# One maximum over sixteen heads and one subtraction: merging two halves in a top-k attention layer

## The chip, the cores and the metric

The kernel runs on one core of one Trainium2 chip. The metric is the device time of one execution in microseconds; a kernel's time is the median of its runs.

## The reference, cut to what matters

The program is a transformer of four layers on `x` of 64 sequences x 128 tokens x 128 features, with a context of 64 x 77 x 128. Each layer adds a cross attention and a feed-forward part, both on the layer-normed `x`. The change lies in the cross attention of the last layer, which has low-rank projections and keeps only the 64 largest of 77 scores:

```python
qh = _heads(_lowrank_proj(q, Uq, Vq, bq), B, L)      # 16 heads of 8
kh = _heads(_lowrank_proj(k, Uk, Vk, bk), B, S)      # S = 77
vh = _heads(_lowrank_proj(v, Uv, Vv, bv), B, S)
scores = jnp.einsum('bhld,bhsd->bhls', qh, kh) * SCALE
flat = scores.reshape(-1, S)
vals, idx = jax.lax.top_k(flat, 64)
p = jax.nn.softmax(vals, axis=-1)
attn = jnp.zeros_like(flat).at[rows, idx].set(p)     # back in shape b h l s
out = jnp.einsum('bhls,bhsd->bhld', attn, vh)
```

The feed-forward part behind it is a mixture of 64 experts; each token goes to its four likeliest, and each expert takes at most 128 of them.

## The kernel before, in words

`attention_layer` works one sequence of 128 tokens per step, tokens on the 128 partitions, and writes 64 such steps out as straight code. Each engine has its own list, and the lists meet only at semaphores. In step `s` an engine works on several sequences at once: the scores of sequence `s`, the selection of `s-1`, the probabilities of `s-2` (`lag` is 2), the output of later stages. The tiles have two halves, taken in turn (`u`), so sequence `s` reuses the buffers of `s-2`.

Sixteen heads of 77 scores are 1232 numbers per token. TensorE puts them into four PSUM banks of four heads. ScalarE copies them in two halves of eight heads (616 numbers) into `a_T` (`copy_scores`, L565, signals `copied0` and `copied1`). VectorE finds the maximum of each head (`subtract_max`, L696, into `a_mx`, signals `mx0` and `mx1`). GpSimd writes "maximum minus score", a distance, over the scores (`distances`, L630, signals `distance0` and `distance1`).

To keep 64 of 77, the 13 largest distances are thrown out, in two rounds of MAX8 (the eight largest of a row) and MATCH_REPLACE8 (put a huge negative number where they stand): `select_eight` (L727), `replace_eight` (L735), `select_rest` (L743), a memset of three of the second eight (L751) and `replace_rest` (L756). Each is 16 instructions, one per head, of 77 elements. TensorE then turns the result, ScalarE takes the absolute value and exp(-distance), and TensorE weighs the values.

VectorE's list in step `s` of this layer is, in order (the names in brackets belong to the router and exist in one step of four):

```
select_eight(s-1), residual(s-4), [minima], replace_eight(s-1),
subtract_max(s, half 0), norm_heads(s-3), select_rest(s-1), place_v(s+1),
[sums | best | keys_in_order], statistics(s-4), [best_four],
subtract_max(s, half 1), [reciprocals | marks], replace_rest(s-1)
```

`norm_heads` (L676, L681) divides the weighed values by the sums of the probabilities; `place_v` (L774) lays out the values of the next sequence.

GpSimd's list in step `s` is: the router's `pool_first`, `distances` for half 0 and half 1, `add_bias` (L618), the router's `pool_end`.

The router of the feed-forward part runs inside these steps, for groups of four sequences. With `c = s // 4` and `v = s % 4`, `pool_first` does `probabilities(c-3)` and `deviations(c-2)` at `v` = 0 and `place(c-3)` at `v` = 2. `place` (L2613 to L2629) computes for each token the row that each chosen expert has for it, and ends in `e3r_skey` (L2626) and `e3r_wf` (L2629). VectorE's `keys_in_order` (L2725) takes the four largest of `e3r_skey` in the same step. `pool_end` does `chosen` at `v` = 0, `fill_rows` at `v` = 2, and in every step a `scatter` (L2645) of four indirect DMAs, at `v` of 0 and 1 from the fifth group of steps on. After the last attention step the router goes on for a few groups alone. The context for each sequence comes by SyncE's DMAs (L314), which wait for `proj`.

Of the kernel before, what the change touches and what calls it, by code (L numbers as in the profile page):

```python
# [9 lines left out]
ALU = mybir.AluOpType  # L10
ACT = mybir.ActivationFunctionType
AX = mybir.AxisListType.X
# [17 lines left out]
def real(i, n=B):  # L30

    return not isinstance(i, int) or 0 <= i < n


def past(i, back):

    return not isinstance(i, int) or i >= back
# [39 lines left out]
def bcast(ap, axis, n):  # L77

    a = ap.unsqueeze(axis)
    shape = list(a.shape)  # L80
    shape[axis] = n
    return a.broadcast_to(shape)
# [45 lines left out]
def attention_layer(nc, m, k, w, heads, keys, scale, context=None, mask=None, topk=0, lowrank=False,  # L128
# [21 lines left out]
    k_ready = "k_by_scalar" if topk else "k"  # L150
    sfree = "copied" if topk else "sfree"
# [4 lines left out]
    q = m.at  # L156
    with ExitStack() as ctx:
# [10 lines left out]
        y = sb("y", [S, 2, D])  # L168
        yT = sb("yT", [D, 2, S])
# [4 lines left out]
        mx = sb("mx", [S, 2, heads])  # L174
        T = sb("T", [S, 2, heads * keys])
        Pr = sb("Pr", [keys, 2, heads * S])
        oT = sb("oT", [D, 2, wide])
# [430 lines left out]
        @block.gpsimd  # L608
        def _(pool):
            norm_gpsimd_rest(pool, m)  # L610
            if y_by_scalar:
                offsets(pool, 2, slice(FIRST, B))

            def add_bias(i, u):
                pool.wait_ge(q["y"], q.nth("y", i))
                xi = m.X[:, bass.ds(i, 1), :].rearrange("p a d -> p (a d)")
                if inner is None:
                    pool.tensor_tensor(xi, xi, bo[:, :], ALU.add).then_inc(q["bias"], 1)  # L618
                else:
                    pool.wait_ge(q["yraw"], q.nth("yraw", i))  # L620
                    pool.tensor_tensor(y0[:, u, :], y0[:, u, :], bo[:, :], ALU.add).then_inc(q["y0"], 1)
                    pool.wait_ge(q["y0"], q.nth("y0", i))
                    pool.tensor_tensor(xi, xi, y0[:, u, :], ALU.add).then_inc(q["bias"], 1)

            def distances(i, u, half):

                t3 = T[:, u, :].rearrange("p (k h c) -> p k h c", k=2, c=keys)[:, half, :, :]
                m3 = mx[:, u, :].rearrange("p (k h) -> p k h", k=2)[:, half, :]
                pool.wait_ge(q[f"mx{half}"], q.nth(f"mx{half}", i))
                pool.tensor_tensor(t3, bcast(m3, 2, keys), t3, ALU.subtract).then_inc(q[f"distance{half}"], 1)  # L630

            def less_maxima(i, u, half):

                t3 = T[:, u, :].rearrange("p (k h c) -> p k h c", k=2, c=keys)[:, half, :, :]
                m3 = mx[:, u, :].rearrange("p (k h) -> p k h", k=2)[:, half, :]
                pool.wait_ge(q[f"mx{half}"], q.nth(f"mx{half}", i))
                pool.tensor_tensor(t3, t3, bcast(m3, 2, keys), ALU.subtract).then_inc(q[f"T{half}"], 1)  # L637

            def step(s, v, h):
                u, a = v % 2, (v + 1) % 2  # L640
                if inner is not None and real(s + 1):
                    pool.wait_ge(q["yT"], q.nth("yT", s + 1))
                    if past(s + 1, 2):
                        pool.wait_ge(q["proj"], q.nth("proj", s + 1, 2))

                    pool.tensor_tensor(yT[:, a, :], xw[:, a, :], m.WIDTH_FEATURES[:, :], ALU.mult) \
                        .then_inc(q["xT"], 1)
                if real(s):
                    if mask is not None:
                        for half in range(2):  # L650
                            less_maxima(s, u, half)
                    if router is not None:
                        router.pool_first(pool, s)
                    if topk:
                        for half in range(2):
                            distances(s, u, half)
                    add_bias(s, u)
                elif router is not None:
                    router.pool_first(pool, s)
                if router is not None:  # L660
                    router.pool_end(pool, s)
            run_written_out(pool, step, 2, max(0, beyond), slots=slots)
            if router is not None:
                router.pool_last(pool)

        @block.vector
        def _(dve):
# [16 lines left out]
            def subtract_max(i, u, h, half):  # L684

                banks = slice(2 * half, 2 * half + 2)
                raw = PS[:, banks, 0:hpg * keys].rearrange("p g (a c) -> p g a c", c=keys)
                t4 = T[:, u, :].rearrange("p (g a c) -> p g a c", a=hpg, c=keys)[:, banks, :, :]
                t3 = T[:, u, :].rearrange("p (k h c) -> p k h c", k=2, c=keys)[:, half, :, :]
                m4 = mx[:, u, :].rearrange("p (g a) -> p g a", a=hpg)[:, banks, :]  # L690
                m3 = mx[:, u, :].rearrange("p (k h) -> p k h", k=2)[:, half, :]
                if topk:
                    dve.wait_ge(q[f"copied{half}"], q.nth(f"copied{half}", i))
                    if past(i, 2):
                        dve.wait_ge(q[f"distance{half}"], q.nth(f"distance{half}", i, 2))
                    dve.tensor_reduce(m3, t3, AX, ALU.max).then_inc(q[f"mx{half}"], 1)  # L696
                    return
                dve.wait_ge(q["scores"], q.nth("scores", i))
                if past(i, 2):
                    turned = f"PT{turns // 2 * (half + 1) - 1}"  # L700
                    dve.wait_ge(q[turned], q.nth(turned, i, 2))
                if mask is not None:
                    dve.wait_ge(q[f"mask{u}"], h * 16 + (16 + mask_base))
                    for g in range(2):
                        last = dve.scalar_tensor_tensor(
                            out=t4[:, g, :, :], in0=bcast(mk[:, u, :], 1, hpg), scalar=-1.0e9,
                            in1=raw[:, g, :, :], op0=ALU.mult, op1=ALU.add)
                    last.then_inc(q[f"sfree{half}"], 1)
                    dve.wait_ge(q[f"sfree{half}"], q.nth(f"sfree{half}", i))
                    if past(i, 2):  # L710
                        dve.wait_ge(q[f"T{half}"], q.nth(f"T{half}", i, 2))
                    dve.tensor_reduce(m3, t3, AX, ALU.max).then_inc(q[f"mx{half}"], 1)  # L712
                    return
                dve.tensor_reduce(m4, raw, AX, ALU.max).then_inc(q[f"mx{half}"], 1)  # L714
                dve.wait_ge(q[f"mx{half}"], q.nth(f"mx{half}", i))
                dve.tensor_tensor(t4, raw, bcast(m4, 3, keys), ALU.subtract).then_inc(q[f"sfree{half}"], 1)  # L716

            def select_eight(i, u):
                t3 = T[:, u, :].rearrange("p (h c) -> p h c", c=keys)


                for h in range(heads):
                    if h % (heads // 2) == 0:
                        half = h // (heads // 2)
                        dve.wait_ge(q[f"distance{half}"], q.nth(f"distance{half}", i))
                        pass_wait()
                    last = dve.max(r1[:, u, 8 * h:8 * h + 8], t3[:, h, :])  # L727
                last.then_inc(q["r1"], 1)
# [63 lines left out]
            def step(s, v, h):  # L792
                u, a = v % 2, (v + 1) % 2
                end, fin = s - lag - 1, s - lag - 2
                if topk:
# [6 lines left out]
                        router.vector_first(dve, s)  # L802
                    if real(s - 1):
                        replace_eight(s - 1, a)
                    if real(s):
                        subtract_max(s, u, h, 0)
                    if real(end):
                        norm_heads(end, (v - lag - 1) % 2)
                    if real(s - 1):
# [7 lines left out]
                    if router is not None:  # L817
                        router.vector_fourth(dve, s)
                    if real(s):
                        subtract_max(s, u, h, 1)  # L820
                    if router is not None:
                        router.vector_last(dve, s)
                    if real(s - 1):
# [25 lines left out]
                    router.vector_last(dve, s)  # L849
            run_written_out(dve, step, 2, max(lag + 2, beyond), slots=slots)  # L850

        used = ["y", "yTps", "yT", "proj", "projv", "q", k_ready, "v", "scores", f"{sfree}0", f"{sfree}1", "mx0", "mx1",
                "pv", "oT", "back", "rec", "O", "OTps", "OT", "out", "bias", "x"]
        used += [f"{n}{g}" for n in ("PT", "P") for g in range(turns)]
        used += ["distance0", "distance1"] if topk else []
        used += ["T0", "T1"] if less_max == "T" else []
        used += ["xT"] if inner is not None else []
        for n in used:
# [2192 lines left out]
def program(nc, t):  # L3051
    with ExitStack() as ctx:
# [3 lines left out]
        def sem(name):  # L3056
# [26 lines left out]
        m.at = Signals(ctx, nc, "at", [  # L3083
# [5 lines left out]
            "y0", "yraw", "irstd", "cut", "mr", "nmr", "in_sq", "in_var", "in_mr", "in_nmr"])  # L3089
# [147 lines left out]
```

## Time and profile before

| | us |
|---|---|
| median of 3 runs | 3944.61 |
| lowest and highest | 3942.61, 3950.3 |
| the profiled execution | 3949.06 |
| its span, first to last instruction | 3947.3 |
| attention of layer 3 in that span, about | 2710 to 3634 |

The profile is that of one execution. Busy time is the time in which an engine worked on instructions; a record can overlap its successor on the same engine, so on an engine without idle time the distance from start to start is what adds up. PE is TensorE, DVE is VectorE, ACT is ScalarE, POOL is GpSimd. An idle time in square brackets stands ahead of the instruction of its line, with the one that released it.

### The profile page before, as it was taken

How to read it: one execution, taken by the hardware profiler on the slowest of the kernel's cores; microseconds unless marked ns; L12 is line 12 of the kernel's file. 1: busy time of each engine (PE TensorE's matmuls, PEld its weight loads, DVE VectorE, ACT ScalarE, POOL GpSimd, SP SyncE). 2: the span in 40 equal slices, each digit the busy share in tenths (PEclk: the TensorE clock that was granted, in tenths of full speed). 3: DMA queues.
4: the chain of work that ended last, by engine and by line, in shares of the span. 5: the costliest groups of instructions: out<-in, count | busy, mean ns of one | idle time of the engine just before them, and what ended most of it. 6: DMA issues, size and time to landing. Idle time of an engine off the chain costs nothing. (4 is left out here: it accounts for less than half of the span.)

```text
span 3947.3 us, 77991 instructions
## 1 busy us (share of the span) xinstructions
PE 3004.5 (76%) x23435; PEld 1888.8 (48%) x23435; DVE 3014.5 (76%) x12267; ACT 2240.8 (57%) x4368; POOL 1905.5 (48%) x2166
## 2 busy tenths in 40 slices
PE   3777776999979997797599968885777767777069
PEld 1222222444447776443467745554555555555046
DVE  6999997666667776344788858887999999998065
ACT  4999997333346665242366646664666666665030
POOL 5777776000014566575444442222256666666660
PEclk9999998999989999898799979996555665655585
DMA  2000000940000010253200000000011100000037
GB/s 74 5 5 5 5 6 22 418 193 0 0 16 17 27 29 26 79 140 111 61 15 15 15 8 2 2 2 13 20 36 38 38 18 5 5 5 2 1 111 213
DMA packets 161015, 177.77 MB, mean 45 GB/s; under 512 B 71762, under 2 KB 136180, under 8 KB 153179
## 3 DMA queue, kind: packets, MB, share of 16 engines
q1 hardware_dynamic: 127964, 140.65, 11.7%
q0 software_dynamic: 23424, 27.94, 2.1%
q10 hardware_dynamic: 9216, 4.20, 0.4%
q8 instruction: 197, 3.23, 0.3%
q14 instruction: 214, 1.75, 0.1%
HBM read 80.48 MB, written 113.61 MB: 49 GB/s over the span
## 5 line engine op out<-in xcount | busy, mean ns | idle before, releaser
L395 PE MATMUL PS<-IDENT,a_T 128*77 128x128 f32 (+1 forms) x3584 | 618.3, 313 | 132.0 <-ACT a_Pr L540 110.5
L1037 ACT ACTIVATE l_H<-l_H 128x2048 f32<-128x2048 f32 (+2 forms) x256 | 597.3, 2702 | 2.8 <-POOL l_H L1089 2.6
L395 PEld LDWEIGHTS PS<-IDENT,a_T 128*77 128x77 f32 (+1 forms) x3584 | 487.0, 171 | 226.8 <-ACT a_Pr L540 88.6
L1089 POOL TENSOR_TENSOR l_H<-l_feat,l_text 128x4096 f32<-128x4096 f32 x64 | 450.4, 7039 | 131.5 <-PE PS L993 130.8
L993 PE MATMUL PS<-l_H,l_wide 128*32 128x512 f32 (+1 forms) x2560 | 332.2, 595 | 165.3 <-ACT l_H L1037 165.3
L1111 DVE TENSOR_TENSOR l_H<-PS,l_text 128x2048 f32<-128x2048 f32 (+1 forms) x192 | 411.7, 2146 | 2.1 <-ACT l_text L1064 2.1
L542 ACT ACTIVATE a_Pr<-PS 77x512 f32<-77x512 f32 (+1 forms) x640 | 375.4, 588 | 59.4 <-PE PS L395 59.4
L412 PE MATMUL PS<-a_Pr,a_vaug 77*32 77x128 f32 (+1 forms) x7168 | 303.9, 316 | 21.8 <-ACT a_OT L571 15.8
L630 POOL TENSOR_TENSOR a_T<-a_mx,a_T 128x616 f32<-128x616 f32 x128 | 155.5, 1215 | 307.4 <-DVE a_mx L696 307.4
L2645 POOL DMA_INDIRECT expert_rows<-e3r_row,e3r_rows_at x256 | 253.6, 991 | 86.7 <-issue 73.6
L109 POOL TENSOR_TENSOR RSTD<-norm_tmp,MINUS_HALF 128x24 f32<-128x24 f32 x6 | 25.1, 4189 | 553.3 <-DVE norm_tmp L102 553.3
L338 PE MATMUL PS<-a_kblk,a_qT 32*128 32x308 f32 (+1 forms) x2048 | 243.1, 549 | 24.2 <-ACT e3r_posc L2515 7.4
L637 POOL TENSOR_TENSOR a_T<-a_T,a_mx 128x616 f32<-128x616 f32 x128 | 155.6, 1216 | 204.0 <-DVE a_mx L712 204.0
L412 PEld LDWEIGHTS PS<-a_Pr,a_vaug 77*32 77x32 f32 (+1 forms) x7168 | 214.1, 125 | 76.2 <-issue 54.2
L528 ACT ACTIVATE a_yT<-PS 128x128 f32<-128x128 f32 x192 | 53.3, 278 | 301.1 <-PE PS L348 301.1
L993 PEld LDWEIGHTS PS<-l_H,l_wide 128*32 128x32 f32 x2560 | 57.5, 109 | 342.7 <-ACT l_H L1037 294.6
L735 DVE MATCH_REPLACE8 a_T<-a_r,a_T 128x77 f32<-128x77 f32 x1024 | 213.6, 222 | 0.3 <-issue 0.3
L756 DVE MATCH_REPLACE8 a_T<-a_r,a_T 128x77 f32<-128x77 f32 x1024 | 213.6, 223 | 0.0
L429 PE MATMUL PS<-IDENT,a_O 128*128 128x128 f32 x256 | 86.1, 336 | 160.0 <-DVE a_O L681 160.0
L714 DVE TENSOR_REDUCE a_mx<-PS 128x8 f32<-128x616 f32 (+1 forms) x256 | 189.2, 739 | 22.9 <-PE PS L338 13.7
L1492 ACT ACTIVATE e_act_g<-PS 128x512 f32<-128x512 f32 x128 | 76.5, 597 | 225.8 <-PE PS L1444 225.6
L716 DVE TENSOR_TENSOR a_T<-PS,a_mx 128x616 f32<-128x616 f32 (+1 forms) x256 | 190.8, 745 | 8.8
(356 smaller groups left out, 7857.7 us busy)
## 6 DMA issues: line engine op xcount, KB each, us to landing
pair_rows<-e_zero SPq DMA_DIRECT2D x35, 1024.0 KB, 25.3
expert_shares<-e_zero SPq DMA_DIRECT2D x16, 1024.0 KB, 25.7
e3c_four<-expert_shares SPq DMA_DIRECT2D x64, 256.0 KB, 3.2
e_xin<-pair_rows SPq DMA_DIRECT2D x39, 264.0 KB, 3.2
e_four<-pair_shares SPq DMA_DIRECT2D x16, 512.0 KB, 4.5
e_w<-in_L_ffn_blocks SPq DMA_DIRECT2D x39, 194.0 KB
e3x_xin<-expert_rows SPq DMA_DIRECT2D x32, 200.0 KB
expert_rows<-e_zero SPq DMA_DIRECT2D x6, 1024.0 KB, 24.8
```

Source lines behind the costliest of these rows:

```text
L338: last = pe.matmul(PS[:, g, 0:hpg * keys], qT[32 * g:32 * g + 32, u, :], kblk[32 * g:32 * g + 32, u, :], start=True, stop=True, tile_posit ...
L395: last = pe.transpose(PS[0:keys, 4 + g % 2, j * S:(j + 1) * S], T[:, u, c:c + keys], m.IDENT[:, :])
L412: last = pe.matmul(PS[32 * j:32 * j + 32, 6, g * S:(g + 1) * S], vaug[:, v, c * 32:c * 32 + 32], Pr[:, u, c * S:(c + 1) * S], start=(p == ...
L542: act.activation(part, turned, ACT.Exp).then_inc(q[f"P{g}"], 1)
L716: dve.tensor_tensor(t4, raw, bcast(m4, 3, keys), ALU.subtract).then_inc(q[f"sfree{half}"], 1)
L735: last = dve.match_replace(t3[:, h, :], r1[:, u, 8 * h:8 * h + 8], t3[:, h, :], FAR)
L756: last = dve.match_replace(t3[:, h, :], r2[:, u, 8 * h:8 * h + 8], t3[:, h, :], FAR)
L993: last = pe.matmul(PS[32 * j:32 * j + 32, 4 + u, 0:cols], wide[:, 32 - r:64 - r], H[:, u, CH * c * S:CH * c * S + cols], start=(r == 0), s ...
L1037: act.activation(cells, cells, ACT.Tanh).then_inc(q[f"tanh{part}"], 1)
L1089: pool.tensor_tensor(H[:, a, lo * S:hi * S].rearrange("p (t f) -> p t f", f=S), bcast(feat[:, a, :], 1, hi - lo), bcast(text[:, a, lo:hi], ...
L1111: dve.tensor_tensor(H[:, u, lo * S:hi * S].rearrange("p (t f) -> p t f", f=S), bcast(PS[:, 1 + u, 0:S], 1, hi - lo), bcast(text[:, u, lo:h ...
L2645: pool.indirect_dma_start(out=m.rows[:, :], out_offset=bass.IndirectOffsetOnAxis(ap=rows_at[:, i % 3, g * K + k:g * K + k + 1], axis=0), i ...
```

## The change

In the top-k layer only. VectorE no longer takes the maxima of heads 0 to 7 ahead of `norm_heads` and those of heads 8 to 15 behind the router's fourth part. One instruction, `find_maxima`, takes those of all sixteen heads, where the second stood; it waits for both copies, `copied0` and `copied1`, and for the subtraction of sequence `s-2`. GpSimd subtracts all 1232 scores in one instruction, where it had two. `select_eight` has one wait in front of its first head in place of two, one ahead of each eight heads, and one semaphore increment less. The signals `distance1` and, in this layer, `mx1` go. No DMA is added, removed or moved in any list.

```diff
--- before.py
+++ after.py
@@ -622,12 +622,11 @@
                     pool.wait_ge(q["y0"], q.nth("y0", i))
                     pool.tensor_tensor(xi, xi, y0[:, u, :], ALU.add).then_inc(q["bias"], 1)
 
-            def distances(i, u, half):
-
-                t3 = T[:, u, :].rearrange("p (k h c) -> p k h c", k=2, c=keys)[:, half, :, :]
-                m3 = mx[:, u, :].rearrange("p (k h) -> p k h", k=2)[:, half, :]
-                pool.wait_ge(q[f"mx{half}"], q.nth(f"mx{half}", i))
-                pool.tensor_tensor(t3, bcast(m3, 2, keys), t3, ALU.subtract).then_inc(q[f"distance{half}"], 1)
+            def distances(i, u):
+
+                t3 = T[:, u, :].rearrange("p (h c) -> p h c", c=keys)
+                pool.wait_ge(q["mx0"], q.nth("mx0", i))
+                pool.tensor_tensor(t3, bcast(mx[:, u, :], 2, keys), t3, ALU.subtract).then_inc(q["distance0"], 1)
 
             def less_maxima(i, u, half):
 
@@ -652,8 +651,7 @@
                     if router is not None:
                         router.pool_first(pool, s)
                     if topk:
-                        for half in range(2):
-                            distances(s, u, half)
+                        distances(s, u)
                     add_bias(s, u)
                 elif router is not None:
                     router.pool_first(pool, s)
@@ -689,12 +687,6 @@
                 t3 = T[:, u, :].rearrange("p (k h c) -> p k h c", k=2, c=keys)[:, half, :, :]
                 m4 = mx[:, u, :].rearrange("p (g a) -> p g a", a=hpg)[:, banks, :]
                 m3 = mx[:, u, :].rearrange("p (k h) -> p k h", k=2)[:, half, :]
-                if topk:
-                    dve.wait_ge(q[f"copied{half}"], q.nth(f"copied{half}", i))
-                    if past(i, 2):
-                        dve.wait_ge(q[f"distance{half}"], q.nth(f"distance{half}", i, 2))
-                    dve.tensor_reduce(m3, t3, AX, ALU.max).then_inc(q[f"mx{half}"], 1)
-                    return
                 dve.wait_ge(q["scores"], q.nth("scores", i))
                 if past(i, 2):
                     turned = f"PT{turns // 2 * (half + 1) - 1}"
@@ -715,14 +707,21 @@
                 dve.wait_ge(q[f"mx{half}"], q.nth(f"mx{half}", i))
                 dve.tensor_tensor(t4, raw, bcast(m4, 3, keys), ALU.subtract).then_inc(q[f"sfree{half}"], 1)
 
+            def find_maxima(i, u):
+                dve.wait_ge(q["copied0"], q.nth("copied0", i))
+                dve.wait_ge(q["copied1"], q.nth("copied1", i))
+                if past(i, 2):
+                    dve.wait_ge(q["distance0"], q.nth("distance0", i, 2))
+                dve.tensor_reduce(mx[:, u, :], T[:, u, :].rearrange("p (h c) -> p h c", c=keys), AX, ALU.max) \
+                    .then_inc(q["mx0"], 1)
+
             def select_eight(i, u):
                 t3 = T[:, u, :].rearrange("p (h c) -> p h c", c=keys)
 
 
                 for h in range(heads):
-                    if h % (heads // 2) == 0:
-                        half = h // (heads // 2)
-                        dve.wait_ge(q[f"distance{half}"], q.nth(f"distance{half}", i))
+                    if h == 0:
+                        dve.wait_ge(q["distance0"], q.nth("distance0", i))
                         pass_wait()
                     last = dve.max(r1[:, u, 8 * h:8 * h + 8], t3[:, h, :])
                 last.then_inc(q["r1"], 1)
@@ -802,8 +801,6 @@
                         router.vector_first(dve, s)
                     if real(s - 1):
                         replace_eight(s - 1, a)
-                    if real(s):
-                        subtract_max(s, u, h, 0)
                     if real(end):
                         norm_heads(end, (v - lag - 1) % 2)
                     if real(s - 1):
@@ -817,7 +814,7 @@
                     if router is not None:
                         router.vector_fourth(dve, s)
                     if real(s):
-                        subtract_max(s, u, h, 1)
+                        find_maxima(s, u)
                     if router is not None:
                         router.vector_last(dve, s)
                     if real(s - 1):
@@ -849,10 +846,10 @@
                     router.vector_last(dve, s)
             run_written_out(dve, step, 2, max(lag + 2, beyond), slots=slots)
 
-        used = ["y", "yTps", "yT", "proj", "projv", "q", k_ready, "v", "scores", f"{sfree}0", f"{sfree}1", "mx0", "mx1",
+        used = ["y", "yTps", "yT", "proj", "projv", "q", k_ready, "v", "scores", f"{sfree}0", f"{sfree}1", "mx0",
                 "pv", "oT", "back", "rec", "O", "OTps", "OT", "out", "bias", "x"]
         used += [f"{n}{g}" for n in ("PT", "P") for g in range(turns)]
-        used += ["distance0", "distance1"] if topk else []
+        used += ["distance0"] if topk else ["mx1"]
         used += ["T0", "T1"] if less_max == "T" else []
         used += ["xT"] if inner is not None else []
         for n in used:
@@ -3083,7 +3080,7 @@
         m.at = Signals(ctx, nc, "at", [
             "prep", "fold", "ctx0", "ctx1", "mask0", "mask1",
             "y", "yTps", "yT", "proj", "projv", "q", "k", "k_by_scalar", "v", "scores", "sfree0", "sfree1",
-            "copied0", "copied1", "distance0", "distance1", "mx0", "mx1", "pv", "oT", "back",
+            "copied0", "copied1", "distance0", "mx0", "mx1", "pv", "oT", "back",
             "rec", "O", "OTps", "OT", "out", "bias", "x", "T0", "T1", "xT", "PT0", "PT1", "PT2", "PT3",
             "P0", "P1", "P2", "P3", "passed", "r1", "t1", "r2", "r2cut", "abs0", "abs1", "abs2", "abs3",
             "y0", "yraw", "irstd", "cut", "mr", "nmr", "in_sq", "in_var", "in_mr", "in_nmr"])
```

## Rows read from the trace of the kernel before

**Rows 1.** The page: busy time of each engine over the whole span.

```profile
PE 3004.5 (76%) x23435; PEld 1888.8 (48%) x23435; DVE 3014.5 (76%) x12267; ACT 2240.8 (57%) x4368; POOL 1905.5 (48%) x2166
```

**Rows 2.** Busy time by stretch (start:end, length, engines, mean clock, DMA), attention of layer 3.

```profile
2710.00:3634.00 924.00, 670.65 (x4653) 493.06 (x4652) 910.77 (x6891) 588.28 (x1365) 530.89 (x767) 0.58 0.06 18
```

**Rows 3.** The waits of VectorE in that stretch: who for whom, us, times, longest.

```profile
DVE a_mx L696 <- ACT a_T L565: 5.0, 1, 5.0
...
DVE a_r L727 <- POOL a_T L630: 0.5, 1, 0.5
```

**Rows 4.** Timeline of VectorE, a step with `place`: start, length, instruction.

```profile
3127.25 2.33 DVE L727 MAX8 a_r<-a_T 128x8 f32<-128x77 f32 x16
...
3133.06 0.78 DVE L696 TENSOR_REDUCE a_mx<-a_T 128x8 f32<-128x616 f32 x1
3133.76 0.24 DVE L676 RECIPROCAL a_rec<-PS 128x16 f32<-128x16 f32 x1
...
3136.68 0.59 DVE L2725 MAX8 e3r_skeytop<-e3r_skey 128x8 f32<-128x64 f32 x4
...
3137.39 0.77 DVE L696 TENSOR_REDUCE a_mx<-a_T 128x8 f32<-128x616 f32 x1
3138.11 0.10 DVE L751 MEMSET a_r<- 128x48 f32 x1
...
3141.69 0.51 DVE L727 MAX8 a_r<-a_T 128x8 f32<-128x77 f32 x3
```

**Rows 5.** Groups by line, VectorE: count, busy us, mean ns, idle before.

```profile
L727 DVE MAX8 a_r<-a_T 128x8 f32<-128x77 f32 x1024 | 149.1, 223 | 0.5 <-POOL a_T L630 0.5
```

**Rows 6.** Timelines of ScalarE and VectorE around the router's exponentials and their sum.

```profile
2857.81 1.05 ACT L2526 ACTIVATE e3r_row<-e3r_nl,e3r_mn 128x64 f32<-128x64 f32 x4
...
2859.89 0.40 DVE L2689 TENSOR_REDUCE e3r_lsum<-e3r_row 128x4 f32<-128x256 f32 x1
```

**Rows 7.** Timeline of GpSimd over the same step and the end of the one before.

```profile
3123.79 1.21 POOL L630 TENSOR_TENSOR a_T<-a_mx,a_T 128x616 f32<-128x616 f32 x1 [2.60 <-DVE a_mx L696]
...
3125.57 0.99 POOL L2645 DMA_INDIRECT expert_rows<-e3r_row,e3r_rows_at  x1 [0.15 <-issue]
...
3130.45 0.87 POOL L2613 TENSOR_SCALAR e3r_near<-e3r_posc 128x256 f32<-128x256 f32 x1
...
3134.61 0.73 POOL L2626 TENSOR_TENSOR e3r_skey<-e3r_near,e3r_far 128x256 f32<-128x256 f32 x1 [0.17 <-POOL e3r_near L2621]
...
3138.23 1.22 POOL L630 TENSOR_TENSOR a_T<-a_mx,a_T 128x616 f32<-128x616 f32 x1 [1.04 <-DVE a_mx L696]
3139.41 0.45 POOL L618 TENSOR_TENSOR X<-X,a_bo 128x128 f32<-128x128 f32 x1
```

**Rows 8.** Groups by line: a narrow and a wide operation of GpSimd.

```profile
L618 POOL TENSOR_TENSOR X<-X,a_bo 128x128 f32<-128x128 f32 x64 | 29.0, 454 | 0.0
...
L1089 POOL TENSOR_TENSOR l_H<-l_feat,l_text 128x4096 f32<-128x4096 f32 x64 | 450.4, 7039 | 131.5 <-PE PS L993 130.8
```

**Rows 9.** The instructions of two lines: count, ns min/median/max, first and last start.

```profile
L2626 POOL TENSOR_TENSOR e3r_skey<-e3r_near,e3r_far x13: 721/726/728, 2897.8 to 3601.5; 128x256 f32<-128x256 f32 x13
...
L2725 DVE MAX8 e3r_skeytop<-e3r_skey x52: 198/209/221, 2903.5 to 3603.9; 128x8 f32<-128x64 f32 x52
```

**Rows 10.** Timelines behind the last step: GpSimd's keys and VectorE's reading of them.

```profile
3650.93 0.72 POOL L2626 TENSOR_TENSOR e3r_skey<-e3r_near,e3r_far 128x256 f32<-128x256 f32 x1 [0.17 <-POOL e3r_near L2621]
...
3651.82 0.61 DVE L2725 MAX8 e3r_skeytop<-e3r_skey 128x8 f32<-128x64 f32 x4 [4.04 <-POOL e3r_skey L2626]
```

**Rows 11.** Timeline of GpSimd behind the last subtraction.

```profile
3633.81 0.86 POOL L2601 TENSOR_SCALAR e3r_mask<-e3r_mark 128x256 bf16<-128x256 f32 x1 [4.08 <-DVE e3r_mark L2715]
```

**Rows 12.** Timelines of VectorE and GpSimd in the first step of the layer.

```profile
2710.83 0.80 DVE L696 TENSOR_REDUCE a_mx<-a_T 128x8 f32<-128x616 f32 x1
2712.11 2.40 DVE L727 MAX8 a_r<-a_T 128x8 f32<-128x77 f32 x16 [0.49 <-POOL a_T L630]
...
2710.75 2.39 POOL L630 TENSOR_TENSOR a_T<-a_mx,a_T 128x616 f32<-128x616 f32 x2 [1.12 <-DVE a_mx L696]
```

## The prediction

> **What bounds the kernel now.** I read the page first, then the busy time by stretch, the waits, and the timelines of the stretch that the change touches. On the page VectorE and TensorE are each busy 76% of the span, so neither bounds the whole [rows 1]. The change touches only the attention layer of layer 3, from about 2710 us to 3634 us. There VectorE is busy 910.8 of 924 us, 98.6%, TensorE 670.7, ScalarE 588.3 and GpSimd 530.9 [rows 2]. Its idle time is 13.2 us in all; of its waits on other engines two stand out, 5.0 us before the first reduction and 0.5 us in the first selection, each once [rows 3]. So in some 64 steps of about 14.5 us VectorE waits for nobody: what it issues is the time. A microsecond taken from VectorE's list comes off the kernel; one taken from GpSimd, ScalarE or TensorE does not; and a new wait of VectorE goes onto the kernel in full. TensorE's mean granted clock in this stretch is 0.58 [rows 2], but nothing of the change lies on TensorE.
>
> **VectorE, the merged maxima.** Two reductions of 616 elements become one of 1232. The first one starts at 3133.06 and the reciprocal behind it at 3133.76: 0.70 us from start to start (the record of 0.78 overlaps its successor). The second takes 0.72 before the memset [rows 4]. What a merge saves is the part that doesn't depend on size. Sixteen MAX8 of 77 elements take 2.33 us, of which the last record is 0.22: (2.33 - 0.22) / 15 = 0.141 us each [rows 4, 5]. Between 77 and 616 elements the slope is (0.70 - 0.141) / 539 = 1.04 ns an element, which leaves 0.70 - 616 x 1.04 ns = 0.06 us fixed. 64 steps x 0.06 = 3.9 us saved. The bounds: 0.05 by the rounding of these rows (3.2 us), and 0.14 if the fixed part is counted from the record's whole length (0.78 - 0.64; 9.0 us). I take 0.06, since start to start is what adds up on an engine without idle time. The removed waits and the one removed semaphore increment I count at nothing: the sixteen MAX8, with such a wait in their middle, take the 2.33 us that 15 equal steps give.
> The Trainium skill, page "VectorE: DVE Perf Modes", section on the TRN2 errata, gives 58 cycles plus one per element for such an operation from SBUF, which at 0.96 GHz is an estimated 0.060 us fixed; the same section says that measured single operations show about 150 cycles, an estimated 0.156 us. By the larger figure the saving would be 10.0 us and the kernel's change -1.4 us. The start-to-start rows speak for the smaller.
>
> **VectorE, the order.** The first reduction also leaves its place in front of `norm_heads`. So `norm_heads`, `select_rest`, `place_v` and the router's `vector_third` run 0.70 us earlier in the step, and the work behind them runs when it did. `select_rest` still has `norm_heads` (the reciprocal and a product) between it and `replace_eight`. What comes 0.70 us earlier must find its inputs. The tightest from ScalarE that I found is the router's `sums`: exponentials end at 2858.86, the sum starts at 2859.89, so 1.03 us of cover, of which 0.33 is left [rows 6]: no cost, and if it were gone, only the part beyond would cost. TensorE and ScalarE get the heads of `norm_heads` earlier, which is worth nothing, since VectorE doesn't wait for them.
>
> **GpSimd, the merged subtraction.** Per step one operation of 1232 elements stands where the second of 616 stood, and the first is gone from ahead of it. How long is it? 128 elements take 454 ns, 616 take 1215 (the record of 1.22 us in [rows 7]), 4096 take 7039 [rows 8]. From 128 to 616 the slope is 1.56 ns an element, which gives 2.18 us for 1232; from 616 to 4096 it is 1.67, which gives 2.25. The 256-element operation of the router at 726 [rows 9] gives a slope of 1.36 and 2.05 us, the low bound; twice 1215, 2.43 us, is the bound above. I take 2.2 us. GpSimd's total falls slightly, but what stands behind the subtraction starts 2.2 - 1.215 = 0.98 us later against the maxima: `add_bias`, `chosen`, `fill_rows`, the four indirect DMAs of `scatter`, and then, in the next step, the router's `probabilities`, `deviations` or `place`.
>
> **Who waits for that.** (a) `select_eight` of the next step. The second reduction ends at 3138.16, the selection starts at 3141.69: 3.53 us [rows 4]. From the maxima's end to GpSimd's start it is 0.07 (3138.16 to 3138.23, [rows 7]), the operation 2.2, back about 0.17: 2.44. Hidden behind `replace_rest`, with 1.1 us to spare. (b) `keys_in_order` of the router, once in four steps, which needs `e3r_skey`. Here GpSimd is not idle: from the subtraction at 3123.79 over the scatter (3125.57) and `place` (3130.45) to `e3r_skey` (3134.61 + 0.73 = 3135.34) it works without a wait, so all of the lateness arrives there [rows 7]. VectorE reads the keys at 3136.68 [rows 4]: cover 1.34 us, of which the semaphore takes 0.17, as the tail shows, where VectorE does wait (3650.93 + 0.72 = 3651.65 to 3651.82, [rows 10]). Covered lateness is thus 1.17 us; the change uses 0.70 of it from VectorE's side, by coming earlier, and 0.98 from GpSimd's. 0.70 + 0.98 - 1.17 = 0.51 us of new wait. There are 13 such groups in the stretch; before the first, no scatter runs ahead and the cover is 2903.5 - 2898.5 = 5 us [rows 9], so 12 pay: 12 x 0.51 = 6.1 us. (c) The end of the layer. GpSimd waits 4.08 us for `e3r_mark` after the last subtraction [rows 11], so 0.98 us of lateness vanishes there.
>
> **The first step.** Nothing yet stands between maxima and selection. The second reduction starts at 2710.83 and the selection runs from 2712.11 to 2714.51, because half 0 is already subtracted when it begins [rows 12]. With the change the reduction starts at 2710.83 too (it waits for the second copy), ends at 2712.27 (0.80 + 616 x 1.04 ns), GpSimd runs 2712.34 to 2714.54, the selection starts at about 2714.70 and ends at 2717.03. That is 2.5 us later, and as VectorE never idles afterwards it is never won back.
>
> **Sum.** -3.9 + 6.1 + 2.5 = +4.7 us. Per 0.1 us of the GpSimd operation it moves by 1.3 us (12 groups and the first step): +2.8 at 2.05, +7.7 at 2.43. The profiled execution has a span of 3947.3 us and took 3949.06, 4.5 us above the median of 3944.61; its differences are applied to the median: 3944.6 + 4.7 = 3949.3 us, +0.12%. A measurement of this kernel (3942.6 to 3950.3 for three runs) can't tell less than 0.2%, 7.9 us, from no change, so the forecast is "no change that can be told", on the slow side.
>
> **Rivals.**
> 1. GpSimd's wide operation costs at least twice the narrow one. Against it: the fixed part in 454 against 1215 ns. For it: a broadcast operand in both, and no row of this shape. At 2.43 us the sum is +7.7; it counts as slower from 2.45 us on. At 2.65, say, it would be 12 x 0.96 + 2.95 - 3.9 = +10.6 us, 3955 us. Chance 0.13. The Trainium skill, page "GPSIMD Engine Reference", section on elementwise work, has about 2.6 cycles an element for two inputs, at 1.2 GHz an estimated 2.67 us for 1232 elements; the 1215 ns for 616 and 7039 for 4096 lie below that rule.
> 2. The keys aren't late: the gaps that the profile puts down to issue in front of the scatter's DMAs close up, or the 0.17 us is not paid. Then the sum is 2.5 - 3.9 = -1.4 us, 3943 us. Against it: that gap is 0.15 us in [rows 7], and the rest of the chain from 3123.79 is work. Chance 0.12.
> 3. VectorE's fixed part is that of the record, 0.14 us: -9.0 + 8.6 = -0.4 us, 3944 us. Chance 0.08.
> 4. The selection itself waits in every step. That needs a GpSimd operation over 3.3 us, or GpSimd late before the maxima: at 3.5 us, 64 x 0.2 + 12 x 1.8 + 3.8 - 3.9, about +34 us. Against it: 1.1 us of cover and GpSimd's wait of 1.04 us for the maxima even in the step with `place` [rows 7]. Chance 0.03.
> 5. Faster by over 7.9 us: that would need 0.26 us saved per step with both losses in place. Nothing in the rows gives it. Chance 0.04, for what I don't see.
>
> The forecast itself has 0.60. Range by its own bounds 3947 to 3953; with rivals 2 and 3, most of rival 1, and the spread of a median of such runs, 3942 to 3957. Slower by over 0.2%: rivals 1 (most of it) and 4 and the spread of the forecast, 0.18. Faster: 0.05. Within: 0.77.
>
> **What the profile after should show.** L696's group of 128 gone, 64 reductions of 128x1232 with a record of about 1.42 us; 64 subtractions of about 2.2 us on GpSimd; VectorE waiting for `e3r_skey` 12 times, about 0.5 us each, and once about 2.4 us before the first MAX8; no wait of the later `select_eight`. Four steps together grow by 0.51 - 4 x 0.06 = 0.27 us. I'm wrong if the waits at the keys are absent or much longer, if other waits of VectorE appear (for the exponentials, for `place_v`), or if the layers that the change doesn't touch move.

## The result

| | kernel before | changed kernel |
|---|---|---|
| median | 3945.69 us (3938.29 to 3950.31, 16 runs) | 3954.38 us (3951.32 to 3957.7, 16 runs) |
| the profiled execution and its span | 3949.06, 3947.3 | 3951.66, 3949.9 |

The ratio is 1.0023, 95% interval [1.0015, 1.0031]: 8.7 us slower, between 5.9 and 12.2. The forecast was 3949.3 us and +4.7 us. The time lies in the range of 3942 to 3957; the sign of the small difference was forecast, its size is about half of what was measured, and the ratio stands on the edge of the 0.2% that I had called "can't be told". Measured a second time, beside other runs of before (changed_again, below), the ratio was 1.0018 [1.0009, 1.0026], +6.6 us.

To see where the time lies, a whole execution is too coarse: between the two profiled executions the layers that nothing touched differ by almost 5 us. So below, **the layer** is the time from the issue of its first weight load (SyncE, `a_U`) to the start of the last MATCH_REPLACE8 of `replace_rest`. It is 947.3 us in the trace of before (2689.8 to 3637.1) and 954.2 in the trace of the changed kernel (2685.0 to 3639.2): +6.9 us.

The page's first part, to be read beside [rows 1]:

```profile
PE 3009.3 (76%) x23435; PEld 1892.8 (48%) x23435; DVE 3012.5 (76%) x12203; ACT 2239.4 (57%) x4368; POOL 1894.5 (48%) x2102
```

VectorE has 64 instructions less and is busy 2.0 us less; GpSimd has 64 less and is busy 11.0 us less. Yet the kernel is slower. Busy time by stretch of the changed kernel, beside [rows 2]:

```profile
2710.00:3637.00 927.00, 673.17 (x4641) 494.91 (x4639) 908.00 (x6833) 586.07 (x1358) 518.84 (x704) 0.57 0.06 18
```

Over a stretch that is 3 us longer VectorE is busy 2.8 us less. So it has 19.0 us of idle time in this stretch, where it had 13.2 in that of [rows 2]. The waits of VectorE in this stretch and its start, largest first (who for whom, total, times, longest), beside [rows 3]:

```profile
DVE a_vaug L773 <- PE PS L367: 7.4, 2, 4.6
DVE e3r_skeytop L2722 <- POOL e3r_skey L2623: 5.7, 12, 0.5
DVE a_r L726 <- POOL a_T L629: 2.5, 1, 2.5
...
DVE a_mx L715 <- ACT a_T L565: 1.2, 1, 1.2
```

Two entries differ from [rows 3]: twelve waits for `e3r_skey`, which are new, and the one in front of the first selection, 2.5 us in place of 0.5. The start also looks different (7.4 us for `place_v`, 1.2 for the copy, where before it was 2.75 and 5.05), but that is mostly the same time put down otherwise: with no reduction of half 0 between them, VectorE waits for the values of sequence 1 first. The sum is 8.6 us in place of 7.8, since the 0.8 us of that reduction were work and are now idle. The groups by line of the two merged operations, VectorE and GpSimd (busy, mean ns, idle before):

```profile
L715 DVE TENSOR_REDUCE a_mx<-a_T 128x16 f32<-128x1232 f32 x64 | 90.9, 1420 | 1.2 <-ACT a_T L565 1.2
```

```profile
L629 POOL TENSOR_TENSOR a_T<-a_mx,a_T 128x1232 f32<-128x1232 f32 x64 | 143.8, 2247 | 327.0 <-DVE a_mx L715 327.0
```

1420 ns and 2247 ns; the forecast had 1.42 us and 2.2 us. A step with `place` in the changed kernel, VectorE and then GpSimd, beside [rows 4] and [rows 7]:

```profile
3121.19 1.41 DVE L715 TENSOR_REDUCE a_mx<-a_T 128x16 f32<-128x1232 f32 x1
...
3132.44 2.33 DVE L742 MAX8 a_r<-a_T 128x8 f32<-128x77 f32 x16
3134.69 0.28 DVE L773 TENSOR_TENSOR a_vaug<-PS,a_bv 77x128 f32<-77x128 f32 x1
3135.45 0.60 DVE L2722 MAX8 e3r_skeytop<-e3r_skey 128x8 f32<-128x64 f32 x4 [0.49 <-POOL e3r_skey L2623]
3135.97 0.27 DVE L787 BATCH_NORM_STATS2 STATS<-X 128x6 f32<-128x128 f32 x1
3136.17 1.42 DVE L715 TENSOR_REDUCE a_mx<-a_T 128x16 f32<-128x1232 f32 x1
```

```profile
3122.68 2.24 POOL L629 TENSOR_TENSOR a_T<-a_mx,a_T 128x1232 f32<-128x1232 f32 x1 [4.28 <-DVE a_mx L715]
3124.89 0.45 POOL L618 TENSOR_TENSOR X<-X,a_bo 128x128 f32<-128x128 f32 x1
3125.50 0.99 POOL L2642 DMA_INDIRECT expert_rows<-e3r_row,e3r_rows_at  x1 [0.16 <-issue]
...
3130.39 0.87 POOL L2610 TENSOR_SCALAR e3r_near<-e3r_posc 128x256 f32<-128x256 f32 x1
...
3134.55 0.72 POOL L2623 TENSOR_TENSOR e3r_skey<-e3r_near,e3r_far 128x256 f32<-128x256 f32 x1 [0.17 <-POOL e3r_near L2618]
...
3137.66 2.25 POOL L629 TENSOR_TENSOR a_T<-a_mx,a_T 128x1232 f32<-128x1232 f32 x1 [1.70 <-DVE a_mx L715]
```

The reader is to follow GpSimd from the subtraction at 3122.68 to `e3r_skey`, which ends at 3134.55 + 0.72 = 3135.27. It waits for no other engine there. It has idle times, of 0.16 and three times 0.30 us in front of the four indirect DMAs, which the profile puts down to issue, and of 0.17 us for a result of its own; the same five are in the trace of before. VectorE is done with `place_v` and stands in front of the keys until 3135.45; in [rows 4] they were read with 1.34 us in hand. The first step, beside [rows 12], VectorE and GpSimd:

```profile
2706.32 1.44 DVE L715 TENSOR_REDUCE a_mx<-a_T 128x16 f32<-128x1232 f32 x1 [1.19 <-ACT a_T L565]
2710.22 2.34 DVE L726 MAX8 a_r<-a_T 128x8 f32<-128x77 f32 x16 [2.47 <-POOL a_T L629]
```

```profile
2707.84 2.25 POOL L629 TENSOR_TENSOR a_T<-a_mx,a_T 128x1232 f32<-128x1232 f32 x1 [2.88 <-DVE a_mx L715]
```

Counted from the first weight load, the selection ends 27.59 us in (2710.22 + 2.34 - 2684.97), against 24.75 before: 2.8 us later. Of this 0.3 is there before the reduction starts (21.35 us in, the second reduction of before 21.07), and as much as that differs between two traces of the changed kernel: from the first weight load to the first selection it is 25.25 us here and 24.98 in the second (changed_again).

### The profile page after: what moved, and what is told of

Read it like the earlier page. It is cut to its first block and busy times, and to the rows that moved or that the text cites. A ratio compares the mean times of both kernels' runs of the same rounds, so it can differ in the third digit from the quotient of the medians.

```text
span 3949.9 us, 77739 instructions
## 1 busy us (share of the span) xinstructions
PE 3009.3 (76%) x23435; PEld 1892.8 (48%) x23435; DVE 3012.5 (76%) x12203; ACT 2239.4 (57%) x4368; POOL 1894.5 (48%) x2102
## 5 line engine op out<-in xcount | busy, mean ns | idle before, releaser
L395 PE MATMUL PS<-IDENT,a_T 128*77 128x128 f32 (+1 forms) x3584 | 619.7, 313 | 143.3 <-ACT a_Pr L540 108.5
L395 PEld LDWEIGHTS PS<-IDENT,a_T 128*77 128x77 f32 (+1 forms) x3584 | 486.4, 172 | 240.6 <-ACT a_Pr L540 87.2
L629 POOL TENSOR_TENSOR a_T<-a_mx,a_T 128x1232 f32<-128x1232 f32 x64 | 143.8, 2247 | 327.0 <-DVE a_mx L715 327.0
L429 PE MATMUL PS<-IDENT,a_O 128*128 128x128 f32 x256 | 85.8, 335 | 150.8 <-DVE a_O L679 150.7
```

The lines of the kernel that those rows point to most:

```text
L395: last = pe.transpose(PS[0:keys, 4 + g % 2, j * S:(j + 1) * S], T[:, u, c:c + keys], m.IDENT[:, :])
```

## The experiments

Each was timed beside runs of the kernel before on the same chip. The first four ran on a chip on which the kernel before takes 4078.56 us (4063.74 to 4087.3, 35 runs). The next four ran on another, where it takes 3948.48 us (3938.62 to 3951.2, 23 runs), the last three on a third, where it takes 3948.26 us (3944.24 to 3951.88, 25 runs). The chip of the result itself is not on record. Where a text says "the second chip" it means the slow one, and by "the first chip" one of those with about 3948 us. Nothing is compared across the chips but the length of the layer, with that said.

**keys_later.** The router's keys are read later in VectorE's step, when GpSimd has them.

```diff
 def vector_third(dve, s):
-    if v == 2 and have(c - 3):
-        keys_in_order(dve, c - 3)
 def vector_last(dve, s):
+    if v == 2 and have(c - 3):
+        keys_in_order(dve, c - 3)
```

> The changed kernel with one edit: the router's keys_in_order moves behind find_maxima in VectorE's step. Theory (GpSimd's lateness of about 1.05 us meets VectorE's earlier reading of the keys): the twelve waits for e3r_skey, 0.55 us each, go; against the kernel before, -3.8 saved + 2.6 in the first step = about -1 us, some 6.6 us below the changed kernel. Rival (the loss comes with the wait for both copies, or lies in layers that the change doesn't touch): still +6 to +9 us above before.

Measured: 4069.86 us, ratio 0.9982 [0.9967, 0.9996]. The waits for the keys are gone from the stretch, the one for the first selection is left:

```profile
DVE a_vaug L773 <- PE PS L367: 7.4, 2, 4.6
...
DVE a_r L726 <- POOL a_T L629: 2.5, 1, 2.5
...
DVE a_mx L715 <- ACT a_T L565: 1.2, 1, 1.2
```

The layer is 948.1 us, 6 us less than in the changed kernel. The rival, that the loss comes with the wait for both copies or lies elsewhere, would have left it near 954, and falls. The ratio is lower than the theory had it (-7 in place of -1 us, the interval reaching to -1.6), while the layer is 0.6 us above that of before on the other chips; what the whole kernel gained on this chip is not in the layer, and I can't say where it is.

**subtraction_only.** The kernel before with GpSimd's merge alone.

```diff
 def distances(i, u):
+    pool.wait_ge(q["mx0"], ...); pool.wait_ge(q["mx1"], ...)
+    pool.tensor_tensor(t3, bcast(mx[:, u, :], 2, keys), t3, ALU.subtract)
 # VectorE's list: subtract_max(s, half 0) and (s, half 1) at their old places
```

> The kernel before with GpSimd's merge alone; VectorE keeps its two reductions at their old places. Theory: GpSimd is as late as in the changed kernel (about 1.05 us), but VectorE reads the keys at its old time with 1.17 us of cover, so no wait for e3r_skey; only the first selection waits, about 2.0 us more; total +2 us. Rival (lateness alone is enough to make VectorE wait, the 0.70 us of reordering plays no part): twelve waits and +6 us or more.

Measured: 4075.08 us, ratio 0.9998 [0.9986, 1.0011]; no wait for the keys in the attention steps, 2.5 us in front of the first selection; the layer 951.0 us. GpSimd is as late here as in the changed kernel, and VectorE doesn't wait. So lateness alone is not enough: it takes VectorE's 0.70 us of coming earlier as well. It is nearly enough, though: in ten of the twelve groups VectorE reads the keys 0.21 to 0.24 us after GpSimd is done, where 0.17 us is the time that it takes when it waits. The layer is 3.5 us above before's, not 2 as expected: 2.1 us lie in the first step, the rest is spread over single steps and has no cause that I know.

**first_split.** Sequence 0 in halves, the rest as in the changed kernel.

```diff
 def distances(i, u):
+    if i == 0:   # half 0 after mx1, half 1 after mx0, one signal each
+        ...
+        return
 # VectorE: for s == 0 a reduction of half 0 ahead of norm_heads, of half 1 at the end
```

> The changed kernel, but sequence 0 is handled in halves as before (two reductions at their old places, two subtractions, two waits). Theory: the 2.5 us of the first step go, the twelve waits for the keys stay: about +3.5 us against before. Rival (the first step's delay is absorbed later, since other things are late there too): no gain over the changed kernel, +6 to +9 us.

Measured: 4072.01 us, ratio 0.9991 [0.9978, 1.0004]; the wait in front of the first selection falls to 0.5 us, the value of [rows 3], the waits for the keys stay (eleven that the profile lists, 4.3 us); the layer 951.3 us.

**both_mended.** Both edits.

> Both edits together: keys_in_order behind find_maxima and sequence 0 in halves. Theory: what is left is the saving of one fixed cost per step, 63 x 0.05 to 0.06, so -3 to -4 us against before (ratio 0.999). Rival (something outside the two losses costs the 2 us by which the changed kernel's measured growth exceeds the sum of its trace): -1 to -2 us or above zero.

Measured: 4068.71 us, ratio 0.9977 [0.9964, 0.999]; the layer 945.4 us. Within the chip the layers fit together: without the keys' waits 5.9 us less (951.3 to 945.4), without the first step's 2.7 less (948.1 to 945.4). By their ratios all four lie 3 to 7 us below what was expected, while the intervals are 10 to 12 us wide; so the next ones have the two kernels themselves beside them.

**same_again.** The kernel before as if it were new.

> The kernel before, unchanged, measured as if it were a new one, to see what the comparison itself can tell and how long the layer is in a second trace. All theories: ratio 1.000 within its interval; from the issue of the layer's first weight load to the start of the last MATCH_REPLACE8 of the attention 947 us, as in the trace of before, 949 if it ran on the second, slower chip.

Measured: 3949.27 us, ratio 1.0002 [0.9993, 1.0011]; the layer 947.6 us. So a ratio can be trusted to about 0.1%, and the layer repeats within 0.3 us.

**changed_again.** The changed kernel beside the same runs.

> The changed kernel, unchanged, beside the same runs of before. Theory (two losses less one saving): the layer is 6 to 7 us longer than in same_again, and the whole kernel by as much, ratio 1.0016. Rival (2 us or more of the measured growth lie outside the layer): the layer grows by 6 to 7, the kernel by 9 or more.

Measured: 3955.06 us, ratio 1.0018 [1.0009, 1.0026]: +6.6 us. The layer alone is 6.8 us longer (954.4 against 947.6), so nothing is left for other layers; the 8.7 us of the first measurement and 6.9 are the same within the interval.

**early_maxima.** The merged reduction at the place of half 0, with sequence 0 in halves.

```diff
 replace_eight(s - 1, a)
+if s == 0: find_first(u, 0)
+elif real(s): find_maxima(s, u)
 norm_heads(end, ...)
```

> The merge with the reduction at the first half's old place, ahead of norm_heads, and sequence 0 in halves. GpSimd then subtracts some 3 us earlier in the step, and VectorE reads the keys 0.64 us later than before. Theory: no wait for the keys although GpSimd's work is as long; one fixed cost per step saved; -3 us against before. Rival (the second copy isn't there yet at the early place, or norm_heads 0.64 us later makes VectorE wait for place_v): waits for copied1 or the projection of the values, up to 0.6 us in one step of four or more, -3 + 10 = up to +7 us.

Measured: 4019.22 us, ratio 1.0189 [1.0175, 1.0204]; the layer 1018.7 us. The rival holds, and its price was far too low: no wait for the keys, but VectorE stands 66.2 us, 46 times, in front of the reduction. The waits of VectorE in this layer begin with:

```profile
DVE a_mx L734 <- issue: 66.2, 46, 3.1
```

The profile names no releaser ("issue"). The start times name it: 45 of these 46 reductions start 0.09 us after the end of a copy by ScalarE (L565). Two successive reductions in the timeline of VectorE, and between them TensorE's and ScalarE's:

```profile
3097.67 1.44 DVE L734 TENSOR_REDUCE a_mx<-a_T 128x16 f32<-128x1232 f32 x1 [2.81 <-issue]
3099.03 0.25 DVE L681 RECIPROCAL a_rec<-PS 128x16 f32<-128x16 f32 x1
...
3114.02 1.44 DVE L734 TENSOR_REDUCE a_mx<-a_T 128x16 f32<-128x1232 f32 x1 [1.41 <-issue]
```

```profile
3099.65 0.47 PE L429 MATMUL PS<-IDENT,a_O 128*128 128x128 f32 x1 [3.07 <-DVE a_O L686]
...
3107.77 1.91 PE L395 MATMUL PS<-IDENT,a_T 128*77 128x128 f32 x8
...
3112.27 0.66 PE L395 MATMUL PS<-IDENT,a_T 128*77 128x128 f32 x4 [1.05 <-ACT a_Pr L540]
```

```profile
3108.87 0.59 ACT L538 ACTIVATE a_Pr<-PS 77x512 f32<-77x512 f32 x1 [0.58 <-PE PS L395]
...
3110.03 0.66 ACT L565 ACTIVATE a_T<-PS 128x616 f32<-128x616 f32 x1
...
3113.27 0.66 ACT L565 ACTIVATE a_T<-PS 128x616 f32<-128x616 f32 x1
```

The second reduction starts at 3114.02, when ScalarE's second copy ends (3113.27 + 0.66 = 3113.93). That copy stands in ScalarE's list behind three pairs of probabilities (L538, L540), which wait for TensorE's turned scores (L395, 3107.77). TensorE came to them from L429 at 3099.65 with no idle time that the timeline lists, and L429 had waited 3.07 us for `a_O`, which `norm_heads` writes, directly behind the reduction of 3097.67. So it is a ring: reduction, `norm_heads`, TensorE's whole list, ScalarE's list, reduction, 16.35 us around (3097.67 to 3114.02), where the same stretch of VectorE's list takes 14.69 in the mended kernel. The ring is read from this trace; no run here opens it again. The narrow reduction needed only ScalarE's first copy, made 3.24 us earlier in the same list (3110.03): that slack kept the ring open.

**four_reductions.** The one reduction in four of four heads.

```diff
+for g in range(4):
+    last = dve.tensor_reduce(mx[:, u, 4 * g:4 * g + 4], t3[:, 4 * g:4 * g + 4, :], AX, ALU.max)
```

> The changed kernel with its one reduction cut into four of four heads each, to measure the fixed cost of an operation by three more of them per step. Theory (0.06 us from start to start): 3 x 64 x 0.06 = 11.5 us on top of the changed kernel, +18 us against before, ratio 1.0045. Rival (0.14 to 0.156 us, the fixed part of a whole record): 27 to 30 us on top, +35 us, ratio 1.009.

Measured: 3967.24 us, ratio 1.0053 [1.004, 1.0066]; the layer 966.6 us, 12.3 more than 954.3 of the changed kernel. 12.3 / 192 = 0.064 us for each of the 192 operations added, and a step without router work takes 14.06 us in place of 13.88, 0.18 / 3 = 0.06. The fixed part counted from a whole record, 0.14 us or more, would have made it 27 us and is excluded.

**maxima_only.** The other half of the change: one reduction, two subtractions behind it.

```diff
+for half in range(2):
+    g = slice(8 * half, 8 * half + 8)
+    pool.tensor_tensor(t3[:, g, :], bcast(mx[:, u, g], 2, keys), t3[:, g, :], ALU.subtract)
```

> VectorE's merge alone, at its place in the changed kernel; GpSimd subtracts in two operations of 616 one behind the other. Theory: GpSimd's pair takes 2.36 us from start to start where the merged one takes 2.21, so it is 0.15 us later still and the twelve waits for the keys grow from 0.55 to 0.70 us each (8.4 us); the first selection starts on half 0, so the first step costs 1.6 us in place of 2.6; the saving stays 3. The layer (first weight load to the start of the last MATCH_REPLACE8) takes 954 to 955 us, +7 us against before: the same as the changed kernel, put together otherwise. Rival (the width of GpSimd's operation is what makes VectorE wait): waits near zero, the layer at 946 to 948 us.

Measured: 3956.86 us, ratio 1.0022 [1.0012, 1.0032]; the layer 956.6 us:

```profile
DVE e3r_skeytop L2727 <- POOL e3r_skey L2628: 7.7, 12, 0.7
...
DVE a_r L731 <- POOL a_T L631: 1.4, 1, 1.4
```

Twelve waits, longer in sum by 2.0 us (0.16 each) than in the changed kernel, as the theory has it: what makes VectorE wait is the moved reduction together with GpSimd's lateness, not the width of GpSimd's operation. The first selection waits 1.0 us less. The layer is 1.6 to 2.6 us longer than expected. Most of that lies in the steps at `v` = 0, which are 1.5 us longer in sum: 0.07 to 0.09 in ten of thirteen, 0.25 in three; two steps at `v` = 1 are 0.2 to 0.3 longer. Why, I can't say.

**keys_only.** The kernel before with the keys' edit alone.

> The kernel before with keys_in_order moved to the end of VectorE's step and nothing else. Theory (before has no wait there): no change, layer 947 us, ratio 1.000. Rival (the mended kernels were fast because this move gains by itself): -3 us or more.

Measured: 3947.89 us, ratio 0.9998 [0.9989, 1.0007]; the layer 947.6 us. The move gains nothing by itself; it only takes away a wait where there is one.

**mended_again.** The kernel of both_mended on the chip of maxima_only and keys_only.

> The kernel of both_mended once more, beside the runs of before of this call. Theory: -3 to -4 us against before, layer 943.5 to 944.5 us if on the first chip, ratio 0.9990 to 0.9993. Rival (the -9 us measured on the second chip was right): ratio 0.998 or below.

Measured: 3946.34 us, ratio 0.9993 [0.9984, 1.0002]; the layer 944.6 us, 2.7 to 3.0 less than before. It is the better version by its layer, in two traces (945.4 on the slow chip); the ratio alone doesn't show it. The rival falls: the 9 us measured on the slow chip is not there.

## Why the prediction came out as it did

The starts of successive steps in VectorE's list give the terms directly. From the start of `replace_eight` to its start in the next step, by `v`, in us (medians of eleven groups, steps 16 to 59; the sums are of the unrounded values):

| | 0 | 1 | 2 | 3 | sum |
|---|---|---|---|---|---|
| before | 15.28 | 13.94 | 14.74 | 14.34 | 58.30 |
| changed | 15.25 | 13.88 | 15.27 | 14.29 | 58.69 |
| changed, second trace | 15.26 | 13.89 | 15.29 | 14.29 | 58.72 |
| mended (mended_again) | 15.25 | 13.89 | 14.69 | 14.29 | 58.11 |

- **VectorE bounds the layer, and every wait of it counts in full: right.** All that changed in its list or its waits is in the length of the layer, to some tenths of a microsecond.
- **Waits for the keys: right in place, number and cause, sized too low.** Forecast 12 x 0.51 = 6.1 us. Shown: twelve, 0.58 to 0.60 us in the typical group (15.27 or 15.29, less 14.69) and less in two, 6.8 and 7.0 us over all twelve in the two traces of the changed kernel. On the slow chip it is 5.9 (first_split to both_mended). GpSimd's operation takes 2.247 us (I took 2.2), so the lateness is 1.03 us and not 0.98 (3122.68 to 3124.89, less the 1.18 of [rows 7]). The few hundredths that are left I didn't break down. Cause: keys_later takes them away, subtraction_only shows that the reordering is needed for them, maxima_only that the merge of GpSimd is not.
- **First step: right.** Forecast 2.5 us, the traces 2.8 and 2.6, the first with 0.3 from ahead of the reduction; keys_later to both_mended takes away 2.7.
- **Saving: the term that was mis-sized most.** Forecast 64 x 0.06 = 3.9 us. The fixed cost is 0.06, as four_reductions shows in the steps without router work. But a group of four saves only 58.30 - 58.11 = 0.19 us: 0.05 to 0.06 in three of the steps, and 0.03 at `v` = 0. There the router's memset of `best_four` stands directly ahead of the reduction, and `marks`, which needs it, directly behind. `marks` starts 1.35 us after the wide reduction and 0.69 after the narrow one (means of thirteen), 0.02 us more than the 616 elements ask for. That is part of what is missing; the rest I didn't break down. Over the layer the saving is 2.7 to 3.0 us, say 2.9, in place of 3.9 (the layer of mended_again against those of three traces without a merge).
- **Sum.** 6.9 + 2.7 - 2.9 = +6.7 us, where the layer grew by 6.9 and 6.8 and 6.1 + 2.5 - 3.9 = 4.7 was forecast. The two larger errors, 1.0 us in the saving and 0.8 in the waits, went the same way. The first measurement of the whole kernel, +8.7, is above that sum within its interval; what it has beyond the layer has no cause shown.
- **`select_eight` hidden in all later steps, the sum of exponentials and `place_v` in time, the end of the layer indifferent: right.** None of these waits is in the changed kernel's list, and GpSimd waits 1.70 us for the maxima even in the step with `place`. A cover that I didn't name is that of the second copy: behind the second selection it is ready, and early_maxima shows the price where it isn't.
- **Chances.** "Within 0.2%" had 0.77 and "slower" 0.18; the two measurements of the changed kernel, 1.0023 and 1.0018, stand on both sides of that bound, so the case is on the line. With the saving as measured, the forecast would have been near +6.

Rival 1 (GpSimd's operation twice as long) and rival 4 fall by the 2247 ns. The 2247 ns is also below the 2.67 us estimated in rival 1 from the Trainium skill, page "GPSIMD Engine Reference", section on elementwise work, about 2.6 cycles an element for two inputs. Rival 2 falls by the twelve waits. It had also misread its rows: it named one gap of 0.15 us in front of the scatter's DMAs, and there are four, 0.15 and three times 0.30 us, in both traces; they didn't close up. Rival 3 falls by four_reductions. The larger fixed part in the Trainium skill, page "VectorE: DVE Perf Modes", section on the TRN2 errata, about 150 cycles, falls with it as the price of one more operation in a row of them; the 0.06 us here is the smaller figure of that section.

## What to carry to other kernels

Merging two instructions on the busiest engine saves one fixed cost, here at most 0.06 us of a 14.5 us step. It also takes an instruction out of an earlier place, and everything behind that place comes earlier by the instruction's whole length, 0.70 us here: look up each input that is needed there and how long it is ready, and on the producer's engine add what the same edit puts in front of it. A loss of 0.6 us at one step of four outweighed a gain of 0.19 over all of them.

When two halves are merged, the first half's early start is lost twice: at the start of the pipeline, where nothing covers it, and wherever the second half's input is late. What was faster here, by 2.7 to 3.0 us, was to merge in the steady steps only and to move the reader of the late result behind the merged work.

## What the runs showed of the hardware that I hadn't expected

The same kernel takes different time on two chips: the mended one has a span of 3944.8 us on the one (mended_again) and 4060.5 on the other (both_mended), at mean granted clocks of 0.838 and 0.831. The attention layer of this case, which VectorE bounds, takes 944.6 and 945.4 us; the first weight load of that layer is issued at 2688.6 and 2776.7 us. So 88 of the 116 us lie ahead of it and 27 behind. Nearly all of the 88 arise in one stretch: VectorE's same instruction is 0.4 us later at 1230.6 us and 86.9 us later at 1928.4. What makes those stages slower wasn't tried.
